# One Trainium2 core: three shared PSUM banks for the first attention, and 128-row operands in the middle stage

## What is computed

```python
x = x + tanh(g_xattn[0]) * L0_xattn(ctx_1024, layernorm(x), mask, ...)
x = x + tanh(g_ffn[0])   * L0_ffn(layernorm(x), router_w, router_b, W1, b1, W2, b2)
x = x + tanh(g_xattn[1]) * L1_xattn(layernorm(x), ctx_1024, Wq, bq, Wk, bk, Wv, bv, Wo, bo)
x = x + tanh(g_ffn[1])   * L1_ffn(layernorm(x), w_gate, w_up, w_down)

# L0_xattn(x=context, latents): 16 heads of 64
xn, lat = layer_norm(context, g1, b1), layer_norm(latents, g2, b2)
q, kv = lat @ Wq, concatenate([xn, lat]) @ Wkv
weight = softmax(where(full_mask, q k^T / 8, -max))      # 2048 queries x 3649 keys
return (weight @ v) @ Wout
# L0_ffn: softmax over 8 experts, the best 2 renormalised; gelu(x W1 + b1) W2 + b2 of each, weighted
# L1_xattn: 16 heads of 16 over the context, k = ctx @ Wk.T + bk, v = ctx @ Wv.T + bv
```

## Time and profile before

| | |
|---|---|
| time, median of 3 runs | 3395.67 us (3392.9 to 3396.04) |
| time of the profiled execution | 3392.96 us |
| its span in the trace | 3391.1 us |
| PE busy | 3001.4 us, 89% |
| DVE busy | 2453.9 us, 72% |
| POOL busy | 2082.1 us, 61% |
| ACT busy | 1817.4 us, 54% |

### The profile page before, as it was taken

The page is one execution under the profiler, slowest core; times in us unless marked ns, Lnnn a source line. Parts: engine busy times, 40 slices in busy tenths (PEclk is TensorE's granted clock), DMA queues, the critical chain, the costliest instruction groups (busy, mean ns, idle before and its releaser), DMA issues. The chain is left out here.

```text
span 3391.1 us, 53618 instructions
## 1 busy us (share of the span) xinstructions
PE 3001.4 (89%) x21696; PEld 1101.4 (32%) x21704; DVE 2453.9 (72%) x3029; ACT 1817.4 (54%) x2033; POOL 2082.1 (61%) x968
## 2 busy tenths in 40 slices
PE   3589999999999999999999999998697799999947
PEld 1223333333333333333333333322354133333324
DVE  5567777778767877778777876782535888888758
ACT  3155445555555545544555555544443588888833
POOL 0077898888888889879888888989510111111022
PEclk9699999999999999999999999999698799999969
DMA  1000000000000000000000000000210100000000
GB/s 59 5 1 1 1 7 1 1 1 7 1 1 7 1 1 7 1 1 7 1 1 1 2 1 1 1 1 1 74 23 13 42 7 6 7 8 6 4 0 26
DMA packets 24536, 28.72 MB, mean 8 GB/s; under 512 B 6431, under 2 KB 21216, under 8 KB 24290
## 3 DMA queue, kind: packets, MB, share of 16 engines
q1 hardware_dynamic: 24290, 25.30, 2.6%
HBM read 17.42 MB, written 2.10 MB: 6 GB/s over the span
## 5 line engine op out<-in xcount | busy, mean ns | idle before, releaser
L413 POOL TENSOR_TENSOR a_acc_p<-a_acc_p,a_prob 128x1024 f32<-128x1024 f32 x704 | 1726.1, 2452 | 299.5 <-ACT a_prob L483 217.8
L543 DVE TENSOR_REDUCE a_part_max<-wide 128x2 f32<-128x1024 f32 x896 | 1088.4, 1215 | 475.6 <-PE wide L713 474.9
L483 ACT ACTIVATE a_prob<-slot,a_mask_bias 128x1024 f32<-128x1024 f32 x928 | 987.6, 1113 | 732.1 <-PE slot L738 712.7
L753 PE MATMUL bank<-a_prob,a_val 128*64 128x512 f32 x3712 | 898.8, 606 | 2.1 <-ACT a_prob L483 2.1
L713 PE MATMUL wide<-a_k_hi,a_q_hi 64*128 64x512 f16 (+1 forms) x2048 | 365.9, 369 | 147.4 <-DVE a_part_max L543 134.9
L1025 ACT ACTIVATE a_prob<-slot,a_mask_bias 128x1024 f32<-128x1024 f32 x416 | 455.4, 1116 | 65.5 <-PE slot L1183 52.2
L1067 DVE TENSOR_REDUCE a_part_max<-wide 128x1 f32<-128x512 f32 x514 | 332.7, 681 | 37.3 <-PE wide L1171 20.4
L753 PEld LDWEIGHTS bank<-a_prob,a_val 128*64 128x64 f32 x3712 | 226.6, 136 | 394.9 <-issue 290.2
L738 PE MATMUL slot<-a_q_hi,a_k_lo 64*128 64x512 f16 x1856 | 353.1, 377 | 0.0
L738 PE MATMUL slot<-a_q_hi,a_k_step_hi 64*128 64x512 f16 x1728 | 328.7, 377 | 2.6 <-ACT a_prob L483 2.5
L738 PE MATMUL slot<-a_q_lo,a_k_step_hi 64*128 64x512 f16 x1728 | 328.3, 377 | 0.0
(11 more groups left out here) (367 smaller groups left out, 3284.6 us busy)
## 6 DMA issues: line engine op xcount, KB each, us to landing
a_w_staged<-in_w SPq DMA_DIRECT2D x8, 384.0 KB, 3.2
x_res<-in_x SPq DMA_DIRECT2D x1, 2048.0 KB, 9.1
a_q_op<-a_hi SPq DMA_DIRECT2D x128, 16.0 KB, 1.8
out_x<-x_res SPq DMA_DIRECT2D x16, 128.0 KB
a_k_op<-mid_k_hi SPq DMA_DIRECT2D x32, 52.0 KB, 2.2
mid_context<-in_ctxt SPq DMA_DIRECT2D x1, 1601.0 KB, 6.6
mid_w_staged<-in_w1a SPq DMA_DIRECT2D x4, 385.0 KB, 4.2
ctx_rows<-in_ctx SPq DMA_DIRECT2D x1, 1536.0 KB
```

The lines of the kernel that those rows point to most:

```text
L413: nc.gpsimd.tensor_tensor(acc, before, prob[:, k % R, :], ALU.add).then_inc(added_p, 1)
L483: nc.scalar.activation(prob[:, k % R, :], m.slot[k % 2][:, :], ACT.Exp, bias=mbias[:, t:t + 1]).then_inc(probs_ready, 1)
L543: nc.vector.reduce_max(part_max[:, w % 2, :, j, c], pairs, AX.X).then_inc(max_used, 1)
L753: ins = nc.tensor.matmul(av[r, :], val[g % 2][:, t, r], prob[:, k % R, h * QB:(h + 1) * QB], start=(t == 0), stop=(t == NT - 1), tile_posi ...
```

## The change

In the first attention the two banks of `wide` and the bank `side` become one pool of three. A class `Banks` goes through the program once, in Python, and gives every use (each half of each pair, sums, outputs, turn, job) the bank that by a table of times comes free first, and remembers the use before it. TensorE then waits, ahead of each use, for the reader of that use before. VectorE reduces the maxima in two halves of 512, with one count of `max_used` each. The sums stay at t=9, but the inversions go to t=10 to 13, the divide to 14, the outputs to 15 and 17 and with them the residuals to 16 and 18; the first output also waits for the divide. Jobs are placed at other steps.

```diff
+class Banks:
+    def __init__(self):
+        self.until, self.last = [-1e9] * 3, [None] * 3
+        self.of, self.before = {}, {}
+
+    def take(self, what, until):
+        b = self.until.index(min(self.until))
+        self.of[what], self.before[what] = b, self.last[b]
+        self.until[b], self.last[b] = until, what
...
-        turns = [(0, 7), (0, 23), (0, 27), (1, 1), (1, 5), (1, 7), (1, 23), (1, 27), (2, 1), (2, 3), (2, 5), (2, 7),
...
+        turns = [(0, 7), (0, 19), (0, 23), (0, 27), (1, 1), (1, 5), (1, 19), (1, 23), (1, 27), (2, 1), (2, 5), (2, 7),
...
-        self.sums_at, self.invert_at, self.pieces, self.divide_at, self.out_at = 9, 12, 4, 16, (17, 19)
+        self.sums_at, self.invert_at, self.pieces, self.divide_at, self.out_at = 9, 10, 4, 14, (15, 17)
...
+        for k in range(S):
+            w, t = divmod(k, NT)
+            if k + a.lead < S:
+                for h in range(2):
+                    banks.take(("max", k + a.lead, h), k + 0.6 + 0.5 * h)
+            if w and t == a.sums_at:
+                banks.take(("sums", w - 1), w * NT + a.divide_at + 1.0)
+            if w and t in a.out_at:
+                banks.take(("out", w - 1, a.out_at.index(t)), k + 2.0)
+            if t == a.turn_at and w + 1 < a.units:
+                banks.take(("turn", w + 1), k + 1.5)
+            if k in a.job_at:
+                banks.take(("proj", *a.job_at[k]), k + 2.0)
...
-                if i < NT - 1:
-                    j, c = divmod(i, a.full)
-                    nc.vector.reduce_max(part_max[:, w % 2, :, j, c], pairs, AX.X).then_inc(max_used, 1)
...
+                for h in range(2):
+                    src = bank("max", n, h)
+                    if i < NT - 1:
+                        j, c = divmod(i, a.full)
+                        nc.vector.reduce_max(part_max[:, w % 2, h, j:j + 1, c], src, AX.X).then_inc(max_used, 1)
...
-                if n:
-                    pe.wait_ge(max_used, n)
+                for h in range(2):
+                    free("max", n, h)
...
```

```diff
-        self.jobs = [(g, kind, c) for g in range(self.groups) for kind in "kv" for c in range(len(self.chunks))]
+        kinds = [("k", 0)] + [("v", g) for g in range(self.groups)] + [("k", g) for g in range(1, self.groups)]
+        self.jobs = [(g, kind, c) for kind, g in kinds for c in range(nc)]
...
-        ones = sb("ones", [2, P], FP16)
+        ones = sb("ones", [P, 512], FP16)
...
-        wt_h, wt_l = sb("wt_hi", [NE, TOK], FP16), sb("wt_lo", [NE, TOK], FP16)
-        pick = sb("pick", [NE, NE, P], FP16)
+        wt_h, wt_l = sb("wt_hi", [P, TOK], FP16), sb("wt_lo", [P, TOK], FP16)
+        pick = sb("pick", [P, NE, P], FP16)
...
+            def k_low(p):
+                g, _, c = a.jobs[p]
+                at, w = a.chunks[c]
+                dve.wait_ge(evacuated, p + 1)
...
+                pe.wait_ge(bias_ready, 1)
...
+                    ins = nc.tensor.matmul(out[:, 0:w], own_bias, ones[:, 0:w], start=False, stop=True)
```

More of the change, by code:

```diff
@@ L298, in stage_latent @@
         mbias = sb("mask_bias", [P, NT])
-        pairs = m.wide[:, :].rearrange("p (h n) -> p h n", h=2)
-        av, side = m.bank
+        av = m.bank[0]
+        shared = [m.wide[:, 0:512], m.wide[:, 512:1024], m.bank[1][:, :]]
         w_loaded, w_scaled, w_split, wo_loaded = sem("w_loaded"), sem("w_scaled"), sem("w_split"), sem("wo_loaded")
@@ L344, in job_read, with read @@
             return [(v_done, vals(g, i - a.nkq))]
-        def side_read(what):
+        def read(what):
+            if what[0] == "max":
+                return [(max_used, 2 * what[1] + what[2] + 1)]
             if what[0] == "turn":
@@ L353, in side_read, with bank @@
             return job_read(*what[1:])
+        def bank(*what):
+            return shared[banks.of[what]]
         def score_bank(w, t, h):
@@ L618, in _ @@
                     max_of(0)
-            shift_of(0)
+                if n == NT:
+                    shift_of(0)
             for w in range(a.units):
@@ L659, in weights, with free @@
                 return part[:, at:at + P]
-            def free_side(what):
-                if what in side_before:
-                    for read in side_read(side_before[what]):
-                        pe.wait_ge(*read)
+            def free(*what):
+                if banks.before[what] is not None:
+                    for done in read(banks.before[what]):
+                        pe.wait_ge(*done)
             def project(g, i):
                 if g:
-                    free_side(("proj", g, i))
+                    free("proj", g, i)
                 elif i >= 4:
-                    for read in job_read(0, i - 4):
-                        pe.wait_ge(*read)
+                    for done in job_read(0, i - 4):
+                        pe.wait_ge(*done)
                 pe.wait_ge(w_split, g + 1)
@@ L771, in outputs @@
                     j = 2 * z + b
-                    ins = nc.tensor.matmul(side[:, b * D:(b + 1) * D], att[:, j * P:(j + 1) * P], wo[g % 2][:, :], start=True, stop=True)
+                    ins = nc.tensor.matmul(bank("out", w, z)[:, b * D:(b + 1) * D], att[:, j * P:(j + 1) * P], wo[g % 2][:, :], start=True, stop=True)
                 ins.then_inc(out_ready, 1)
@@ L1804, in _ @@
                 route(b)
-            for p in range(4, 12):
+            for p in range(NC, NC + a.routing):
                 project(p)
-            first(0)
-            first(1)
-            project(12)
-            project(13)
             pe.wait_ge(weights_done, 1)
@@ L1817, in _ @@
                 ins.then_inc(wt_turned, 1)
-                project(14 + g)
-            for p in range(14 + NB, a.nj):
+                project(NC + a.routing + g)
+            first(0)
+            first(1)
+            for p in range(NC + a.routing + NB, a.nj):
                 project(p)
```

224 lines of the change are left out of this document (109 added, 115 removed).

## The result

The changed kernel takes 3512.97 us (3512.37 to 3515.01, 4 runs) beside 3394.98 for the kernel before in the same series: ratio 1.0349, interval 1.0331 to 1.0367, +118 us. The forecast was 3537 in a range of 3430 to 3605. The profiled execution took 3515.01 us, its span is 3513.0.

What follows compares the result with a forecast made beforehand. TensorE, with its waits for VectorE's reductions, was taken to bound the first attention. Profiled 3393.0 + 125 (waits) + 39 (clock) − 14 (lead) − 1 (tail) − 8 (middle stage) = 3534, plus 2.7 to the median: 3537 us, range 3430 to 3605.

Steps and rivals of the forecast that it cites:

- The mechanism: First attention's steps: pairs inheriting a bank wait for VectorE's last use of it; with the moved steps, +125 us.
- walk: Step-by-step timing of a first-attention unit in VectorE's order, t=8 to 22: waits sum to 9.25 us with jobs at 7, 19.
- The clock: First attention: longer idle before t=13 drops TensorE to 1.2 GHz behind it in each of 31 units, +39 us (0 to 53).
- the prediction's own sign: First attention: the forecast is wrong if idles of 2.7 us leave the clock at 1.00.
- The lead: 33 pairs before step 0: with halves and three banks a chained pair follows after 1.38 us instead of 1.93, −14 us.
- The middle stage: Stage after the first attention: value blocks and expert loop shorten, together −8 us (−20 to +5).
- the gains of 2 and 6: Middle stage: 2 us taken of 10 from shorter value blocks, 6 us from 128-row operands in the expert loop's 32 steps.
- the +3 for the bias of the keys: Middle stage: 16 added bias matmuls for keys cost 3 us.
- the +2 for the bias chain: Middle stage: VectorE's bias chain ahead of the first job costs 2 us.
- Faster: First attention: third bank frees TensorE from VectorE, decided by the divide ending before TensorE reaches t=15; 3299 us, chance 0.10.
- The milder loss: First attention: same waits without clock fall, 3498 us, or waits half as large, 3455; chance 0.13.
- third rival: First attention: much slower, waits keep TensorE at 1.2 GHz for longer stretches, 3640 us; chance 0.08.

Runs made afterwards that it cites:

- Experiment 4: Changed kernel with 0.3 added in the table to the times at which sums, outputs, turns and jobs give back their bank: 3408.49 us (1.005).
- experiment 12: Changed kernel with VectorE adding tile 13 in place of tile 9, so the add of t=11 comes at t=15: 3416.01 us (1.0063).
- experiment 2: Kernel before with only the change's steps for inversions, divide, outputs and jobs; separate bank and whole reductions stay: 3414.13 us (1.0063).
- Experiment 9: Kernel before with the new middle stage, but operands of the weights and b2 cut from 128 to 8 rows: 3388.35 us (0.9979).
- Experiment 6: Changed kernel with the steps of before and 0.3 added to the times at which other uses give back a bank: 3369.08 us (0.9931).

## Why the prediction was right, and where its sizes were off

**The mechanism** held: pairs that inherit a bank wait for divide, residuals and splits. Experiment 4, which changes nothing but banks, gave 101 us, about 80 of them by these waits. The other part of the loss lies at t=11 to 14, beside the inversions and the add: 77 of the 144 us by which the steps grew. That the inversions cost there was forecast too, and experiment 12 shows how much hangs on the one add. The idle on the pair's line is 287 us, forecast 270. Waits of the first unit whose walk the prediction gives, forecast and measured:

| t | 9 | 11 | 12 | 13 | 15 | 17 | 19 | 21 | t=8 to 22, pair to pair |
|---|---|---|---|---|---|---|---|---|---|
| forecast, us | 0.88 | 0.25 | 0.7 | 2.8 | 1.0 | 0.9 | 1.45 | 1.26 | 39.7 |
| measured, us | 1.01 | 0.90 | 0.30 | 1.78 | 0.94 | 1.0 | 1.22 | 0.95 | 38.5 |

**The adds** were the terms of wrong size inside a right sum. I took the durations of rows 5 in VectorE's order for every unit, 1.6, 2.2, 2.7 and 2.9. Measured in the first unit they are 2.49, 1.31, 2.36 and 1.33, in the second 2.57, 3.05, 1.55 and 1.55. So t=13 waits 1.8 us in the first unit and 3.3 in the second, where the walk had 2.8, and t=19 1.0 to 1.2 instead of 1.45; the errors nearly cancelled. Without the clock falls the steps grew by 143.8 − 15.4 = 128 us, the forecast said 125. That this sum came out so near is partly luck: experiment 2 has nearly the same instructions on VectorE around t=11 (reductions whole instead of halved) and an add of 1.20 there.

**The clock** was over-sized: +39 forecast, +15 measured. In the traced run TensorE's clock falls eleven times in the steps: behind t=13 in all seven second units that the pattern covers and in three of seven last ones, each time after 3.16 us of idle, and once in the last group, after 1.90. What a fall costs was well sized: 1.4 to 2.2 us in the second unit (4 times 1.4, 3 times 2.2), 1.6 in the last (3 times), 1.5 in the last group. That makes 18.5 us, and the two falls of the trace before had cost 3.1. The wrong step was "each unit", and it has two parts. First, the idle before t=12 and 13 came out at 1.6 to 1.8 us in first and third units, where I had forecast 2.7, since the adds there were short; no fall follows an idle that short in the steps of any trace. Second, a fall is not certain behind a longer idle. In the steps of all fourteen traces, one of the kernel before and thirteen of the others, a fall to 0.50 came behind 15 of 25 idles of 1.90 to 1.92 us, behind one of 2.46, and behind 23 of 28 of 3.16; what decides in a single case stays unexplained. This is the eleventh fall, with its idle, and the clock behind it in the columns of rows 8:

```profile
2403.89 0.37 PE L743 MATMUL bank<-a_k_hi,a_q_hi 64*128 64x512 f16 x1 [1.90 <-DVE a_part_max L572]
```

```profile
2404.80:2408.10 3.30, 3.30 (x12) 0.61 (x10) 1.92 (x4) 0.00 (x0) 3.07 (x2) 0.50 0.00 0
```

By the prediction's own sign, idles of 2.7 us that leave the clock at 1.00, this part failed in four of the fourteen idles of 3.16 us in the changed kernel. The rule of the Trainium skill that the prediction weighed, clock lost only behind long gaps ("TensorE: Matmul & The Clock Gate", "Why this matters for your kernels"), does not hold here as a strict one either: the falls behind 1.9 us are against it, and so are the five idles of 3.16 us with none. That the longer idle is followed by a fall more often is in its direction.

**The lead** gave 11 us, not 14: the period is 1.49 us, not 1.38, since 0.88 of idle follow matmuls of 0.60, and the pair behind the turn waits 2.08 us for `a_shift` (before, 1.32 for the reduction, as the pairs around it). Timeline of TensorE there:

```profile
124.66 0.58 PE L743 MATMUL bank<-a_k_hi,a_q_hi 64*128 64x512 f16 x1 [0.88 <-DVE a_part_max L572]
...
126.15 0.58 PE L743 MATMUL wide<-a_k_hi,a_q_hi 64*128 64x512 f16 x1 [0.88 <-DVE a_part_max L572]
...
156.11 0.58 PE L743 MATMUL bank<-a_k_hi,a_q_hi 64*128 64x512 f16 x1 [2.08 <-DVE a_shift L589]
```

**The middle stage**: −10.6, forecast −8. The 8 are only the gains of 2 and 6; the +3 for the bias of the keys and the +2 for the bias chain, which the prediction prices, are missing from it. With them its terms give −3, and the whole forecast would have been 3542. The expert loop is 7.7 us shorter (−6 forecast): 5.4 in its 29 regular steps, and 2.2 in the first two, which before the change ran longer at the half clock. Experiment 9 confirms the cause for the steps. A value block takes 0.39 instead of 0.60 us, forecast 0.40:

```profile
2569.97 0.22 PE L1785 MATMUL wide<-mid_bias_op,mid_ones 128*128 128x128 f16 x1
...
2570.36 0.22 PE L1785 MATMUL wide<-mid_bias_op,mid_ones 128*128 128x128 f16 x1
```

Of these 10 us only some 3 appear before the expert loop begins (83.4 us into the stage instead of 86.4), about as forecast, for two reasons that the traces show. The first job starts 3.4 us later in the stage (22.8 against 19.4). It stands idle behind the bias chain:

```profile
2548.98 1.01 PE L1776 MATMUL wide<-ct_hi,mid_kv_hi 128*128 128x512 f16 x2 [5.99 <-DVE mid_bias_op L1658]
```

But before the change it had an idle of 5.32 in the same place, behind GpSimd's `ct_lo`, so only 0.7 of the 3.4 us is idle that came in here. The other 2.8 arose ahead of it, where the normalisations on VectorE took longer; why is not shown. And TensorE stands idle once more ahead of the first expert step, now for the low half of the keys, which the change moved from GpSimd to VectorE. Before, then after:

```profile
2480.39 0.37 PE L1774 MATMUL slot<-mid_wt_hi,mid_pick 8*128 8x512 f16 x1 [0.46 <-ACT a_val L1507]
```

```profile
2609.57 0.59 PE L1809 MATMUL slot<-mid_wt_hi,mid_pick 128*128 128x512 f16 x1 [4.28 <-DVE mid_k_lo L1643]
```

No run puts that low half back on GpSimd, so what it would give is open.

**The rivals.** "Faster" decided, as the prediction put it, at the divide against t=15; it came 0.8 us late. Experiment 6, with late banks and old steps, is a faster kernel at 3369, but not by that rival's mechanism: of its 75 us in the steps nothing appears (2128.4 us against 2127.1), and the gain is that of lead and middle stage. The milder loss (no falls) would be some 3495. The price of the third rival, 3640, does not follow from its terms: 31 x 4 are 124 us, which on top of 3537 make 3661 and on top of 3498 make 3622. Neither came near, since the clock fell in eleven of 31 units and cost 1.4 to 2.2 us each time.

**Open** is what decides on which side of GpSimd's add VectorE's falls in each unit; the experiments show that it changes with the order, and I could not forecast it. Open too is why the clock falls behind one idle and not behind another of the same length.

## What to carry to other kernels

In this kernel the pool saved waits only where a bank's next user came well after its reader: a pair that took the bank in the very next step put that reader on TensorE's path. The table had decided this by 0.1 step: it gave a job's bank back at 2.0 and the last pair's second bank at 2.1. Where a table of guesses lies so close between two candidates, ask what each costs when its reader is last in its engine's list. And price an instruction that competes with another engine by both ends of its duration, then place it where the critical engine waits anyway.

## What the runs showed of the hardware

- Adds of 128 x 1024 float32 from two SBUF operands took 1.20 to 3.40 us on VectorE over all traces, by how much of a GpSimd add was left to run when they came. In the changed kernel all 128 ended 1.08 to 1.09 us after such an add of GpSimd; in experiment 2 the 14 that came before it took 1.20 us. GpSimd's next one is then 3.13 to 3.15 us long instead of 2.35 in the two cases shown.
- A clock fall to 0.50 followed 23 of 28 idles of 3.16 us on TensorE, 15 of 25 of 1.90 to 1.92 us, and none of 1.6 to 1.8 us, in the steps of fourteen traces. One fall cost 1.4 to 2.2 us in the changed kernel.
- Matmuls of 8 and 128 rows are busy equally long (0.38 us for 512 columns), but each change of shape adds about 0.1 us ahead and behind; for blocks of 128 columns this was 0.60 against 0.39 us for seven matmuls.
